# Prefill of a four-layer graph kernel: the second bias is added by TensorE into the second product's bank, and VectorE adds x to that bank

## The reference

```python
x = _layernorm(x + _L0_gnn_ref(x, edge_index, W1, b1, W2, b2))   # two GCN convolutions, relu between
x = _layernorm(x + _L1_gnn_ref(...))                              # mean over 8 relations, root, bias
x = _layernorm(x + _L2_gnn_ref(...))                              # attention over edges
x = _layernorm(x + _L3_gnn_ref(...))                              # sum over 16 relations, relu
```

## Time and profile before

| | us |
|---|---|
| median of 3 runs | 3284.75 (3284.0 to 3285.56) |
| the profiled execution | 3286.39 |
| its span | 3284.5 |
| TensorE, VectorE, ScalarE, GpSimd busy, share of the span | 73%, 74%, 52%, 62% |
| mean granted TensorE clock | 0.86 of full speed |

### The profile page before, as it was taken

The page is one execution under the profiler, slowest core; times in us unless marked ns, Lnnn a source line. Parts: engine busy times, 40 slices in busy tenths (PEclk is TensorE's granted clock), DMA queues, the critical chain, the costliest instruction groups (busy, mean ns, idle before and its releaser), DMA issues. The chain is left out here.

```text
span 3284.5 us, 54882 instructions
## 1 busy us (share of the span) xinstructions
PE 2406.4 (73%) x9989; PEld 1510.1 (46%) x9990; DVE 2417.2 (74%) x7453; ACT 1707.0 (52%) x4719; POOL 2024.7 (62%) x1982
## 2 busy tenths in 40 slices
PE   2676664777746666799996666677354999999996
PEld 1444443666546555344443333566243444444443
DVE  7998864788869898699994111333787888888886
ACT  1776775899847777466664444454485111111111
POOL 2777774777477774777774775776001466666663
PEclk9998887999968887899997998555555999999998
DMA  1666554555446665455554777898354111111110
GB/s 50 217 216 198 175 175 135 158 171 171 159 128 189 192 186 166 116 155 148 156 149 142 263 264 230 276 285 277 102 175 145 36 44 49 46 52 50 51 54 29
DMA packets 316465, 490.98 MB, mean 149 GB/s; under 512 B 63594, under 2 KB 143497, under 8 KB 316378
## 3 DMA queue, kind: packets, MB, share of 16 engines
q1 hardware_dynamic: 250266, 377.40, 35.5%
q0 software_dynamic: 66112, 112.69, 12.9%
HBM read 260.66 MB, written 233.07 MB: 150 GB/s over the span
## 5 line engine op out<-in xcount | busy, mean ns | idle before, releaser
L1358 PE MATMUL bank<-sum_masked,sum_w 128*128 128x512 f32 x1568 | 691.3, 594 | 1.4 <-DVE sum_masked L1448 1.4
L1221 POOL DMA_INDIRECT sum_rows<-t_x,m_row_int x196 | 223.6, 1141 | 453.5 <-POOLq L118 239.3
L1448 DVE SCALAR_TENSOR_TENSOR sum_masked<-sum_typ,sum_col 128x512 f32<-128x512 bf16 x784 | 488.9, 685 | 19.2 <-ACT sum_col L1294 17.1
L1358 PEld LDWEIGHTS bank<-sum_masked,sum_w 128*128 128x128 f32 x1568 | 291.4, 191 | 332.3 <-issue 267.7
L1358 PE MATMUL bank<-mean_masked,mean_w 128*128 128x512 f32 x784 | 377.4, 611 | 18.0 <-DVE mean_masked L1448 18.0
L1294 ACT ACTIVATE sum_col<-bank 128x512 f32<-128x512 f32 x49 | 29.3, 597 | 578.7 <-PE bank L1404 565.2
L1221 POOL DMA_INDIRECT mean_rows<-t_x,m_row_int x196 | 220.1, 1123 | 94.7 <-issue 59.4
L1240 POOL DMA_INDIRECT out_dram<-sum_new,m_last_int x196 | 218.9, 1117 | 87.8 <-issue 58.2
L1448 DVE SCALAR_TENSOR_TENSOR mean_masked<-mean_typ,mean_col 128x512 f32<-128x512 bf16 x392 | 249.9, 680 | 19.8 <-ACT mean_col L1294 19.6
L1665 POOL DMA_INDIRECT at_xs<-t_x,at_order x204 | 192.6, 944 | 94.4 <-issue 61.9
L1221 POOL DMA_INDIRECT c_rows<-t_g,m_row_int x196 | 188.4, 961 | 96.5 <-issue 57.3
(11 more groups left out here) (322 smaller groups left out, 5844.1 us busy)
## 6 DMA issues: line engine op xcount, KB each, us to landing
t_hu<-at_made SPq DMA_DIRECT2D x51, 512.0 KB
pf_xc<-x_dram SPq DMA_DIRECT2D x98, 256.0 KB, 3.1
t_g<-pf_g SPq DMA_DIRECT2D x98, 256.0 KB, 3.3
t_x<-pf_x SPq DMA_DIRECT2D x98, 256.0 KB
c_dense_x<-t_x SPq DMA_DIRECT2D x98, 256.0 KB
t_x<-c_dense_x SPq DMA_DIRECT2D x98, 256.0 KB
c_same<-p_same SPq DMA_DIRECT2D x98, 128.0 KB, 3.5
t_g<-c_new SPq DMA_DIRECT2D x49, 256.0 KB
```

The source lines that it names most:

```text
L1221: pool.indirect_dma_start(rows[:, s % 2, j, :], None, source, bass.IndirectOffsetOnAxis(ap=index[:, k:k + 1], axis=0))\
L1358: pe.matmul(H[q][:, :], w[:, r, :], masked[:, r % MASKS, :], start=(r == 0), stop=(r == n_rel - 1))\
L1448: v.scalar_tensor_tensor(out=masked[:, r % MASKS, :], in0=typ[:, q, :], scalar=float(r), in1=col[:, q, :], op0=ALU.is_equal, op1=ALU.mult) ...
```

## The change

TensorE gets one more product per chunk: in step c, behind the transposes, a product of a row of ones (`m.ones[0:1, :]`, the weights) with one row of b2 repeated four times (one partition x 512 columns). It is added (start=False) onto the U bank that holds the second product of chunk c-2, and it waits until ScalarE has copied that bank to `g1`, since `g1` is stored without the bias. VectorE's `xb` goes; its remaining sum reads the bank and `xc` instead of `g1` and `xb`, and waits for a new semaphore `b2_added` instead of `g1_ready`. The second product now waits for `z1_ready` of the chunk that used its bank before instead of `g1_ready`, and only the first of its four pieces starts the bank anew.

```diff
-        xb = sb("xb", [P, BT, D])
...
+        b2_row = m.b2[0:1, :].unsqueeze(1).to_broadcast([1, BT, D])
...
+                s = c - 2
+                if runs(s, 0, END):
+                    pe.wait_ge(g1_ready, s + 1)
+                    pe.matmul(U[q][:, :], m.ones[0:1, :], b2_row, start=False, stop=True, skip_group_check=True)\
+                        .then_inc(b2_added, 1)
                 s = c - 1
                 if runs(s, 0, END):
                     pe.wait_ge(hT_ready, s + 1)
                     if runs(s, 2, END):
-                        pe.wait_ge(g1_ready, s - 1)
+                        pe.wait_ge(z1_ready, s - 1)
                     for j in range(BT):
                         last = pe.matmul(U[o][:, j * D:(j + 1) * D], hT[:, o, j * D:(j + 1) * D], m.w2[:, :],
-                                         start=True, stop=True)
+                                         start=(j == 0), stop=True, skip_group_check=True)
...
-                v.tensor_tensor(xb[:, :, :], xc[:, slot], m.b2_rows, ALU.add).then_inc(xb_ready, 1)
-                v.wait_ge(xb_ready, s + 1)
-                v.wait_ge(g1_ready, s + 1)
+                v.wait_ge(b2_added, s + 1)
                 if runs(s, 2, END):
                     v.wait_ge(x1_ready, s - 1)
-                v.tensor_tensor(z1[:, q], g1[:, q], xb[:, :, :], ALU.add).then_inc(z1_ready, 1)
+                v.tensor_tensor(z1[:, q], U[q][:, :].rearrange("p (b d) -> p b d", d=D), xc[:, slot], ALU.add)\
+                    .then_inc(z1_ready, 1)
```

More of the change, by code:

```diff
@@ L525, in prefill_stage @@
         g1_stored, x1_stored = pair("g1_stored"), pair("x1_stored")
-        x_turned, xT_copied, xw1_done, hT_ready, hw2_done, g1_ready, xb_ready, z1_ready, x1_ready = (
-            sem(n) for n in ("x_turned", "xT_copied", "xw1_done", "hT_ready", "hw2_done", "g1_ready", "xb_ready",
+        x_turned, xT_copied, xw1_done, hT_ready, hw2_done, g1_ready, b2_added, z1_ready, x1_ready = (
+            sem(n) for n in ("x_turned", "xT_copied", "xw1_done", "hT_ready", "hw2_done", "g1_ready", "b2_added",
                              "z1_ready", "x1_ready"))
```

## The result

The changed kernel took 3307.16 us (median of 4 runs, 3298.59 to 3311.58) against 3284.69 us before: a ratio of 1.0065, 95% interval 1.0044 to 1.0086, so slower by 22 us between the medians. The profiled execution is the quickest of the four, 3298.59 us, with a span of 3296.7 us; it understates the loss. The prediction was 3278, range 3264 to 3291.

The account below looks back on a forecast made before the run. It took a ring over two chunks as the bound, with VectorE's limit close in the first half. At full clock 9.3 us gained, less 2.3 for half clock, left 7.0: from 3284.75 to 3278 us, range 3264 to 3291.

Parts of the forecast that it names:

- The ring over two chunks: Prefill cycle of z1, load, x1 store, its landing, x1, g1 and z1 two chunks later: 9.45 us for two chunks.
- The full-clock price of the product: Bias product on TensorE between g1 and z1: 1.02 us, putting z1 1.87 us behind g1's start instead of 2.23.
- the signs of being wrong: In the profile: no t_x wait before x1, ScalarE waiting before most hT, half-length product, or z1 over 2.2 us behind g1.
- the half clock: Bias product at 1.2 GHz, 0.89 us longer: 6.8 us lost if the clock stays, a third, 2.3 us, taken.
- The full-clock gain: Whole prefill with TensorE at full clock: 9.3 us gained, from 6.8 + 3.4 + 0.6 + 0.5 - 2.0.
- chunks up to 45: First half, some 44 chunks: 4.55 us a chunk against 4.70, so 6.8 us gained.
- The table: Table of nodes, mid-prefill: z1 of chunk 48 starts at about 310.9 instead of 308.87, 2.0 us lost once.
- The 16 chunks behind: Steps behind the table of nodes: 4.33 us a chunk against 4.54, so 3.4 us gained.
- Late chunks: Last 28 chunks of the prefill: 4.45 us a chunk against 4.47, so 0.6 us gained.
- the end: Last chunk of the prefill: g1 to z1 is shorter there, 0.5 us gained.
- TensorE becomes the bound: Rival: TensorE's step of 4.2 to 4.3 us, divided by the mean clock, passes 4.70 in the first half: 3300, chance 0.15.
- The clock does not rise: Rival: slow products stand on the ring and cost 6.8 us, leaving 2.5 gained: 3282, chance 0.20.

Follow-up runs that it names:

- e5: The kernel before, with SP's store of x1 placed ahead of the load in each step: 3265.79 us, ratio 0.9942.
- e1: The changed kernel with the bias product over 128 rows (weights 1/128) instead of one: 3290.14 us, ratio 1.0008 to the kernel before.
- e7: The changed kernel with a short bf16 bias product and SP's store of x1 ahead of the load: 3243.99 us, ratio 0.9877 to the kernel before.
- e4: The kernel before, with the one-row product added on TensorE but written to a bank nobody reads: 3296.66 us, ratio 1.003.
- e9: The kernel before, with an added product over 128 rows that nobody reads: 3284.37 us, ratio 0.9998.
- e6: The changed kernel, one-row product kept, with SP's store of x1 ahead of the load: 3245.24 us, ratio 0.9884 to the kernel before.
- e10: The changed kernel again, unaltered, in a later series: 3308.71 us, ratio 1.008 to the kernel before.
- e8: The changed kernel with the bias product ahead of the same step's transposes instead of behind them: 3313.19 us, ratio 1.0087 to the kernel before.
- e2: The changed kernel with b2 as three bf16 parts added by one bf16 product of 65 rows: 3268.02 us, ratio 0.994 to the kernel before.
- e3: The changed kernel without the bias product, b2 left out of the sum: 3262.37 us, ratio 0.9924 to the kernel before.

## Why the prediction was wrong

**What held.** The ring over two chunks was read rightly and e5 shows it, though in the first half VectorE held the pace and the ring stood just under it. The full-clock price of the product was near: 1.12 us for 1.02, z1 1.95 behind g1 for 1.87. Of the signs of being wrong, z1 far behind g1 showed, in the slow chunks. The two that would make TensorE's whole step the bound did not: x1 still waits for the store of t_x, and from 108 to 285 us ScalarE waits for the first product before hT in only 6 chunks, 6.8 us in all. At full clock (e1) a chunk took 4.58 and 4.45 us in the first and the late stretch, where I had 4.55 and 4.45. The sum from the bank costs nothing: 692 ns, where the one from SBUF took 694. The Trainium skill, VectorE: DVE Perf Modes, section on the TRN2 errata, has a larger fixed cost from PSUM; the measurement does not agree. One slip changed nothing: 4.70 - 0.81 is 3.89, not 3.97, for VectorE alone; e7, with VectorE holding the pace in the first half, has 4.06.

**The step that failed is the clock.** I wrote that "the product fills a part of TensorE's idle time" and took 2.3 us for the half clock, with 6.8 us if nothing changed. It did not fill it in a way that raised the clock, and both terms were mis-sized, for two reasons:

1. The product has one row. With it TensorE is 87% busy late and has 0.87; with 128 rows, 0.97 (e1), and unread 0.87 against 0.95 (e4, e9). The product takes the same time with either; the granted clock does not come out the same. I had weighed busy shares only. The Trainium skill, TensorE: Matmul & The Clock Gate, section on what's actually happening, says that activity releases the throttle. This case agrees for products of 128 rows and for e6's dense order; that one row counts for less where TensorE pauses is what e4 against e9 shows.
2. I priced a slow spell at 0.89 us, the stretch of the bias product alone. But z1 then waits for everything ahead of it in TensorE's order: a slow chunk has z1 3.2 us behind g1 instead of 1.95, so 1.25 us, up to 2.5 (z1 of chunk 68 came 4.42 us behind). The ring goes over two chunks, so 9 x 1.25 / 2 over 28 chunks is 0.20 us a chunk, the rise from 4.45 to 4.65. For e10's late part the same sum gives 0.25 of a rise of 0.32, so it is an estimate and not the whole.

From e1 to the changed kernel this makes 16.7 us at the last z1 (540.71 - 523.97) in the profiled executions, 17 to 19 between the medians and 19 to 24 by the ratios, where I had 2.3.

**The full-clock gain was mis-sized too.** I had 9.3 us; e1 has 527.01 - 523.97 = 3.0 at the last z1, and its time shows none. By term: chunks up to 45 gave 4.2 instead of 6.8, as the first eight gained nothing and lost 0.45. The table cost 3.3 (chunks 45 to 48) instead of 2.0; in the changed kernel z1 of chunk 48 waits 3.02 us for TensorE. The 16 chunks behind gave 1.3 instead of 3.4: their pace is 4.46, not the 4.33 that I took from one quiet pair. Late chunks gave 0.5 of 0.6 and the end 0.2 of 0.5. Both steps together: 14.4 us of clock and 6.3 of gain that was not there turn 7.0 gained into the 13.7 lost of this execution.

**The rivals.** "TensorE becomes the bound" had the right side and the right direction, with 3300 and 0.15. That its number came near is in part luck: I had the mean clock dividing TensorE's whole step and 13 us lost in the first half, with the late part even, while the loss came in single slow spells on the ring, and in e10 all of it behind the first half. "The clock does not rise" had the mechanism and too small a price.

**What stays open.** How e1's 3 us at the last z1 came to nothing in its time. From the first gather of the next stage to the end of the span it took 2752.0 us against 2747.3 before; over all thirteen traces this part lies between 2744.0 and 2752.0. And the chip of e1 is the slower one, by some 2.7 us in the kernel before, so a part may be the chip. Only one row and 128 were compared for the same product; where between them the clock turns was not tried, nor other places for the product than e8's, nor why the rows count at all. The loss was not split between pace and queue in e8.

## What to carry to other kernels

Work moved to TensorE is priced by its clock as well as by its columns. Where TensorE pauses, a product of one row fills time but did not keep the clock as the one of 128 rows did (e1, e9), so try it over all rows, or short in bf16 (e2). When an engine's instruction goes on a ring, price everything ahead of it in its engine's order at the slow clock, not the instruction alone. And look first at what holds the ring: moving one store ahead of a waiting load was worth 19 us alone. With the change it made 40 us over the kernel before, though the change by itself lost 22.

## What the runs showed of the hardware

- Two float32 products of 512 columns, nearly equal in length (663 and 649 ns a record) and at the same place, left the granted clock of the late part at 0.87 with one row and at 0.97 with 128 (the changed kernel and e1), and unread at 0.87 and 0.95 (e4 and e9). Busy share alone, 87% against 76% in the first pair, would have said the opposite. Where TensorE had no pauses, one row went with 1.00 (e6).
- The changed kernel spreads over 13 us in its first four runs and 20 in the next six (3302.03 to 3322.54), the kernel before over 2 to 8 in the several series, and e6 over 5. In e4 the slower executions are those of lower clock (0.856 to 0.859 against 0.861 to 0.866). What makes the spread was not shown further: e3, without the product, spreads over 9 us, and e1 over 8.
